# Edge sets sorted in groups of 1, 2, 2, 2 and 1 over later stretches of steps, and the residual scaled by GpSimd in the node phase

## The reference

```python
def gnn(h, src, edge_attr):                    # h = layernorm(x)
    node_feat = relu(h @ W_down.T + b_down)    # 256 -> 64
    time_feat = relu(edge_attr @ W_time.T + b_time)   # 32 -> 64, for every edge
    sums, counts = segment_sum(time_feat, src), segment_sum(1, src)
    mean = sums / maximum(counts, 1)
    fused = relu(concat(node_feat, mean) @ W_fusion.T + b_fusion)
    return h + (fused @ W_up.T + b_up)

x1 = x + gnn(layernorm(x), src, edge_attr)
out = x1 + ffn(layernorm(x1))                  # shared MLP + the best 2 of 4 experts
```

## Time and profile before

| | |
|---|---|
| median of 3 runs | 2168.73 us (2162.14 to 2173.69) |
| the profiled execution | 2177.41 us, of which the span of its trace is 2175.5 us |
| TensorE busy (PE) | 2000.5 us, 92% of the span |
| its weight loads (PEld) | 1672.3 us, 77% |
| VectorE (DVE) | 1779.5 us, 82% |
| ScalarE (ACT) | 1404.0 us, 65% |
| GpSimd (POOL) | 1069.4 us, 49% |
| transfers | 323.68 MB, 149 GB/s in the mean |
| chain that ended last | PE 71%, DVE 11%, DMA 5%, ACT 5%, issue 4% |

### The profile page before, as it was taken

How to read it: one execution, slowest core, us unless ns; L and a number is a source line. 1 busy time by engine, 2 the same in 40 slices (tenths; PEclk the granted TensorE clock), 3 DMA queues, 4 the chain that set the end, 5 groups by cost and what they waited for, 6 DMA issues and landing times.

```text
span 2175.5 us, 75498 instructions
## 1 busy us (share of the span) xinstructions
PE 2000.5 (92%) x26922; PEld 1672.3 (77%) x26946; DVE 1779.5 (82%) x5883; ACT 1404.0 (65%) x3239; POOL 1069.4 (49%) x918
## 2 busy tenths in 40 slices
PE   4788888999999999999999999677869999999998
PEld 1576776799988899999899999677756667666666
DVE  9788999899988999998788887688966767767675
ACT  2598898999989888888988887000014444444443
POOL 0577777778787777787777776100011111111110
PEclk7699999999999999999999999899989999999999
DMA  2244343677766677776778776676731111212110
GB/s 85 71 127 122 126 126 122 189 213 208 211 198 180 205 219 220 217 217 200 208 226 245 239 223 183 178 205 184 205 96 44 53 58 44 66 44 66 44 54 31
DMA packets 239411, 323.68 MB, mean 149 GB/s; under 512 B 42144, under 2 KB 213965, under 8 KB 238706
## 3 DMA queue, kind: packets, MB, share of 16 engines
q1 hardware_dynamic: 176564, 192.90, 32.6%
q0 software_dynamic: 41504, 103.41, 13.0%
q10 hardware_dynamic: 20970, 22.54, 3.7%
HBM read 186.34 MB, written 175.77 MB: 166 GB/s over the span
## 4 chain that ended last, share of the span: by engine, by line
PE 71%; DVE 11%; DMA 5%; ACT 5%; issue 4%; SPq 1%; DVEq 1%; ACTq 1%; POOL 1%; POOLq 0%
PE moved L686 16%; PE bank L715 15%; PE bank L803 10%; PE bank L672 7%; PE moved L816 7%; PE bank L690 4%; DMA arena<-table 3%; DVE arena L1133 2%; PE bank L843 2%; DMA table<-arena 2%; DVE arena L1134 2%; PE bank L699 2%; ACT arena L1590 1%; DVE arena L1334 1%; ACT arena L1596 1%
## 5 line engine op out<-in xcount | busy, mean ns | idle before, releaser
L1812 POOL DMA_INDIRECT table<-arena x832 | 970.3, 1166 | 377.2 <-issue 262.3
L1596 ACT ACTIVATE arena<-moved 128x588 bf16<-128x588 f32 x832 | 547.0, 662 | 108.2 <-PE moved L686 91.7
L686 PE MATMUL moved<-arena 128*128 128x196 bf16 x4992 | 590.5, 254 | 7.8 <-ACT arena L1596 6.7
L686 PEld LDWEIGHTS moved<-arena 128*128 128x128 f16 x4992 | 453.6, 98 | 79.8 <-ACT arena L1596 19.1
L1590 ACT ACTIVATE arena<-bank 128x512 f32<-128x512 f32 x624 | 371.0, 595 | 84.0 <-PE bank L672 68.0
L1235 DVE TENSOR_TENSOR sums<-sums,bank 128x130 f32 x816 | 232.0, 284 | 109.4 <-PE bank L715 88.9
L715 PE MATMUL bank<-arena 128*128 128x64 bf16 (+1 forms) x7344 | 273.4, 194 | 37.2 <-DVE sums L1235 24.6
L715 PE MATMUL bank<-arena,w_all 128*128 128x64 bf16 (+1 forms) x7344 | 272.4, 194 | 19.4 <-DVE sums L1235 18.9
L1711 ACT ACTIVATE arena<-bank,w_all 128x512 f32<-128x512 f32 (+1 forms) x225 | 152.8, 679 | 207.8 <-PE bank L803 116.6
L715 PEld LDWEIGHTS bank<-arena 128*128 128x128 bf16 x7344 | 254.7, 98 | 41.7 <-DVE arena L1215 41.7
L715 PEld LDWEIGHTS bank<-arena,w_all 128*128 128x128 bf16 x7344 | 254.2, 98 | 23.8 <-DVE w_all L1215 23.7
(11 more groups left out here) (292 smaller groups left out, 2864.8 us busy)
## 6 DMA issues: line engine op xcount, KB each, us to landing
arena<-table SPq DMA_DIRECT2D x672, 147.0 KB
arena<-in_attr SPq DMA_DIRECT2D x208, 144.0 KB
arena<-table ACTq DMA_DIRECT2D x144, 147.0 KB
table<-arena POOLq DMA_INDIRECT x832
...
```

The lines of the kernel that those rows point to most:

```text
L686: mm = e.matmul(moved8[:, 4 * (n % 2) + h, 0:PW], slot_hot[s % NSLOT][:, t, h * P:(h + 1) * P], upper(s, 0, PW)[:, t, :], start=j == 0, st ...
L1596: e.activation(row_buf[n % NROWS], moved8[:, 4 * (n % 2):4 * (n % 2) + 3, 0:PW], ACT.Copy).then_inc(s_rows, 1)
L1812: e.indirect_dma_start(out=table, out_offset=bass.IndirectOffsetOnAxis(ap=dest[s % NDEST][:, a:a + 1], axis=0), in_=row_buf[n % NROWS].rea ...
```

## The change

Two things change.

1. **The sorts.** The five sorts take 1, 2, 2, 2 and 1 sets instead of 1, 1, 2, 2 and 2. The second sort keeps its window (steps 1 to 19) and now has two sets in it; the third moves from steps 22 to 45 to steps 26 to 71, the fourth from 51 to 97 to 77 to 123, the last from 103 to 149 to 129 to 175 and has one set.
2. **The residual.** `x_ln`, its 98 stores and ScalarE's `xs_a` go. VectorE's `1 + r` and `s` of all tiles stay in SBUF (`rs_one`, `shift_all`). In the node phase SyncE reloads a group's tiles from `x`, the kernel's input, and GpSimd scales them, one `tensor_scalar` of 128x256 a tile, waits for its own result and then adds the bias as before. A load of a node tile in the loop now waits for the normalised tile in place of `xs_a`; the statistics write their unused output to `passed`; and `fused_a` has one buffer, whose next write waits for the previous store.

The code behind the sorts loses three lines, so that L1133 becomes L1130 and so on.

```diff
-SETS_OF_SORT = (1, 1, 2, 2, 2)
+SETS_OF_SORT = (1, 2, 2, 2, 1)
...
-        sort_windows = [None, (1, 20), (22, 46), (51, 98), (103, 150)]
+        sort_windows = [None, (1, 20), (26, 72), (77, 124), (129, 176)]
...
                         if a >= NXA:
-                            e.wait_ge(s_xs_a, a - NXA + 1)
+                            e.wait_ge(s_xn_a, a - NXA + 1)
...
-                    if name == "keep_x":
-                        e.wait_ge(s_xs_a, a + 1)
-                        e.dma_start(x_ln[g * P:(g + 1) * P, t * D:(t + 1) * D], xs_a).then_inc(s_xln[a % 2], 16)
...
             def load_xs(g):
                 if g >= 2:
                     e.wait_ge(s_x1, landed_x1(g - 2))
-                e.dma_start(xs[g % 2][:, 0:nt[g], :].rearrange("p t d -> p (t d)"), x_ln[g * P:(g + 1) * P, 0:nt[g] * D]).then_inc(s_xln_in[g % 2], 16)
+                full, r0 = full_tiles(g), g * TN * P
+                if full:
+                    e.dma_start(xs[g % 2][:, 0:full, :], x[r0:r0 + full * P, :].rearrange("(t p) d -> p t d", p=P)).then_inc(s_xs_in[g % 2], 16)
...
-                        e.activation(xn_a, xa[a % NXA], ACT.Identity, bias=shift_a[j % 2][:, i:i + 1], scale=rs_a[j % 2][:, i:i + 1]).then_inc(s_xn_a, 1)
-                        if a:
-                            e.wait_ge(s_xln[(a - 1) % 2], 16 * ((a - 1) // 2 + 1))
-                        e.activation(xs_a, xa[a % NXA], ACT.Identity, bias=shift_a[j % 2][:, i:i + 1], scale=rs_one[j % 2][:, i:i + 1]).then_inc(s_xs_a, 1)
+                        e.activation(xn_a, xa[a % NXA], ACT.Identity, bias=shift_all[:, a:a + 1], scale=rs_a[j % 2][:, i:i + 1]).then_inc(s_xn_a, 1)
...
-                        if j >= 2:
-                            e.wait_ge(s_fused_out[j % 2], 32 * (j // 2))
-                        e.activation(fused_a[j % 2], bank[MB][:, 256:384], ACT.Identity, bias=b_f).then_inc(s_fused_a, 1)
+                        if j:
+                            e.wait_ge(s_fused_out[(j - 1) % 2], 32 * ((j - 1) // 2 + 1))
+                        e.activation(fused_a, bank[MB][:, 256:384], ACT.Identity, bias=b_f).then_inc(s_fused_a, 1)
...
             def add_up_bias(g):
-                e.wait_ge(s_xln_in[g % 2], 16 * (g // 2 + 1))
+                e.wait_ge(s_xs_in[g % 2], landed(g, x_dmas))
                 xs_g = xs[g % 2][:, 0:nt[g], :]
+                for t in range(nt[g]):
+                    a = g * TN + t
+                    ins = e.tensor_scalar(xs_g[:, t, :], xs_g[:, t, :], rs_one[:, a:a + 1], shift_all[:, a:a + 1], ALU.mult, ALU.add)
+                ins.then_inc(s_xs_scaled, 1)
+                e.wait_ge(s_xs_scaled, g + 1)
                 e.tensor_tensor(xs_g, xs_g, b3r(b_u, nt[g], D), ALU.add).then_inc(s_xs_up, 1)
```

More of the change, by code:

```diff
@@ L91, in gnn_ffn @@
     fused_dram = nc.dram_tensor("fused_node", (NG * P, TN * P // 2), f32, kind="Internal").ap()
-    x_ln = nc.dram_tensor("x_ln", (NG * P, TN * D), f32, kind="Internal").ap()
     with ExitStack() as ctx:
@@ L109, in gnn_ffn @@
         s_x = [sem(f"s_x_in{i}") for i in range(NXA)]
-        s_xln = [sem(f"s_xln{i}") for i in range(2)]
-        s_xln_in = [sem(f"s_xln_in{i}") for i in range(2)]
+        s_xs_in = [sem(f"s_xs_in{i}") for i in range(2)]
         s_out = [sem(f"s_out{i}") for i in range(2)]
@@ L196, in gnn_ffn @@
         waiting = sb("waiting", [1, 1], f32)
-        ARENA = 31648
+        rs_one = sb("rs_one", [P, NT], f32)
+        shift_all = sb("shift_all", [P, NT], f32)
+        ARENA = 31440
         arena = sb("arena", [P, ARENA], f32)
@@ L290, in gnn_ffn @@
         xn_a = carve([D], f32)
-        xs_a = carve([D], f32)
+        passed = carve([D], f32)
         xt_a = [carve([K, P], f32) for _ in range(2)]
         nf_a = carve([P], f32)
-        fused_a = [carve([P], f32) for _ in range(2)]
+        fused_a = carve([P], f32)
         less_mean = [carve([2], f32) for _ in range(2)]
@@ L298, in gnn_ffn @@
         rs_a = [carve([2], f32) for _ in range(2)]
-        rs_one = [carve([2], f32) for _ in range(2)]
-        shift_a = [carve([2], f32) for _ in range(2)]
         used_1 = top[0]
@@ L418, in gnn_ffn @@
         node_at = {}
-        NODE_STEPS = {"load": 0, "stats": 1, "root": 2, "inverse": 3, "normed": 6, "keep_x": 7, "transposes": 7, "evacuate": 7, "down": 8, "down_relu": 8, "fuse": 9, "keep": 9, "store": 10}
+        NODE_STEPS = {"load": 0, "stats": 1, "root": 2, "inverse": 3, "normed": 6, "transposes": 7, "evacuate": 7, "down": 8, "down_relu": 8, "fuse": 9, "keep": 9, "store": 10}
         PAIRED = ("root", "inverse", "down", "down_relu", "fuse", "keep", "store")
@@ L588, in sync_program @@
                         for i in range(2):
[L589 removed]
+                            e.dma_start(fused_dram[row:row + A, i * P:(i + 1) * P], fused_a[i * A:(i + 1) * A]).then_inc(s_fused_out[j % 2], 16)
             for k, n in last_turns:
@@ L597, in load_xs @@
                     e.wait_ge(s_x1, landed_x1(g - 2))
-                e.dma_start(xs[g % 2][:, 0:nt[g], :].rearrange("p t d -> p (t d)"), x_ln[g * P:(g + 1) * P, 0:nt[g] * D]).then_inc(s_xln_in[g % 2], 16)
+                full, r0 = full_tiles(g), g * TN * P
+                if full:
+                    e.dma_start(xs[g % 2][:, 0:full, :], x[r0:r0 + full * P, :].rearrange("(t p) d -> p t d", p=P)).then_inc(s_xs_in[g % 2], 16)
+                if full < nt[g]:
+                    e.dma_start(xs[g % 2][0:rows[g][-1], full, :], x[r0 + full * P:N, :]).then_inc(s_xs_in[g % 2], 16)
                 if g >= 2:
@@ L606, in sync_program @@
             e.wait_ge(s_added, N_LOADS * CL)
-            for a in range(NT - 2, NT):
-                e.wait_ge(s_xln[a % 2], 16 * (a // 2 + 1))
             for j in range(NT // 2 - 2, NT // 2):
```

19 lines of the change are left out of this document (9 added, 10 removed).

## The result

The changed kernel took 2179.97 us in the median of 15 runs (2174.17 to 2188.04), beside 2168.74 us of 15 runs of the kernel before: a ratio of 1.0055, with a 95% interval of 1.0043 to 1.0067. It is slower by some 11 us. That lies in the predicted range (2159 to 2187), just beyond the 0.5% that I called the bound of a measurable change, and the sum of +3.7 us held only a third of it.

What follows compares the result with a forecast made beforehand. Bounds by stretch: VectorE in steps 1 to 7, 15 to 19, 29 to 35; ScalarE in 49 to 56; TensorE in 57 to 91 and the node phase. Sum +5.3 - 1.5 - 1.2 + 1.1 = +3.7 us: 2172.4, range 2159 to 2187.

Steps and rivals of the forecast that it cites:

- steps 1 to 7, 8 to 14, 15 to 19: Early main loop: more sort rows on VectorE cost +2.4 (+1.0 to +4.4), +0.8 (0 to 3), +3.8 us (2.5 to 5).
- steps 20 to 28: Main loop: 12.1 us fewer sort rows gain nothing, since TensorE's own 5.88 us a step stays: 0.
- steps 29 to 35: Main loop: fewer sort rows on VectorE, which sets the pace, give back -4.2 us (-6.9 to -1.5).
- steps 36 to 48: Main loop: sort rows ahead of size rows in steps 45 to 48 cost +1.0 us (0 to 2.1).
- steps 49 to 56, with the activation: Main loop, ScalarE full: one activation fewer saves time, limited by VectorE's added sort rows: -1.5 us (-3 to 0).
- steps 57 to 156, with the store's wait: Main loop: dropped stores' wait gives -1.2 us; TensorE, full in steps 77 to 91, absorbs lag there, 0 (0 to 3).
- steps 157 to 160: Before turns begin: 13.1 us more sort rows make VectorE 3.5 late, partly covered by a table-load wait: +1.5 us (0 to 3.5).
- step 207 to the second group: Node phase start: GpSimd's four scalings delay the first group by +1.1 us (0 to 2.1); later groups 0.
- Rival A: Node phase: GpSimd blocks VectorE in every group, deciding from about 0.63 us a scaling; about 2190 us, chance 0.10.
- Rival B: Early sort costs all 17.1 us of steps 1 to 19, only 1.5 return; +16.5 us, 2185, chance 0.10.
- Rival C: Relief reaches further: all 6.9 us return in steps 29 to 35, scatter waits vanish (-8); -11.1, 2157.6 us, chance 0.14.

Runs made afterwards that it cites:

- the second trace of before: The kernel before, run once more unchanged for a second trace: 2170.72 us.
- those steps charged: Changed kernel with 18 units of planner work added to every step from 49 on without a turn, so fewer sort rows stand there: 2175.49 us, ratio 1.0012.
- The doubled scalings: Changed kernel with each of the 98 GpSimd scalings followed by a second that multiplies by one and adds nothing: 2200.38 us in one run.

## Why the prediction was right in its range and short in its sum

I subtract the second trace of before from the trace after: 9.2 us in all. Outside the table lie -0.2 us in steps 161 to 206, -1.7 behind the second group, and the roundings.

| term | forecast | traces |
|---|---|---|
| steps 1 to 7, 8 to 14, 15 to 19 | +2.4, +0.8, +3.8 | +4.2, +0.9, +3.8 |
| steps 20 to 28 | 0 | +3.1 |
| steps 29 to 35 | -4.2 | -6.0 |
| steps 36 to 48 | +1.0 | -2.2 |
| steps 49 to 56, with the activation | -1.5 | +0.9 |
| steps 57 to 156, with the store's wait | -1.2 | +2.8 |
| steps 157 to 160 | +1.5 | +3.7 |
| step 207 to the second group | +1.1 | +0.2 |

*Right:* VectorE sets the pace in the early stretches, steps 15 to 19 pay their rows, steps 29 to 35 give back (within my bound of 6.9), the groups stay 22.4 us apart, and a scaling lies under 0.63 us.

*Luck:* that the time lies in the range. The range was wide, and the misses have both signs: steps 1 to 7, 20 to 28, 49 to 76 and 157 to 160 cost more than I had, steps 29 to 48 gave 5.0 us more.

*The step that failed* is how I set each stretch's extra rows against the idle time of the same stretch. Lateness isn't paid there. It is carried on to the first instruction for which TensorE needs VectorE, and the clock that TensorE loses behind the wait comes on top, for which I had no term. For steps 1 to 7 I let steps 6 and 7 take up almost half of the 4.4 us; 4.2 were paid, 3.1 of them in step 7. For "Steps 20 to 28: TensorE's own 5.88 us stays: 0" the sort ran on into step 20 and its first count came late: a wait of 2.1 us and some 1.2 by the clock, +3.1. For steps 157 to 160 I more than halved a lateness of 3.5 us, because VectorE had waited 3.90 us for a table load there; TensorE waited 3.1 and lost some 1.3 by the clock, less the 0.9 that the activation gave there (21.9 to 20.9 with the residual alone): +3.7.

Relief was carried on in the same way. For steps 36 to 48 I counted only the new rows in steps 45 to 48, +1.0, and -2.2 came. VectorE was busy 38.4 of 52.0 us in steps 36 to 44, before 47.9 of 52.6, so it came to the size phase of step 46 earlier: the wait of 3.5 us for its first rows fell to 0.9, and 2.4 were added at the next phase. These are TensorE's waits for VectorE from 330 to 376 us, around steps 45 to 48, before and then after.

```profile
PE bank L641 <- DVE arena L957: 3.5, 1, 3.5
```
```profile
PE bank L644 <- DVE arena L996: 2.4, 1, 2.4
PE bank L638 <- DVE arena L954: 0.9, 1, 0.9
```

For steps 49 to 56 the activation gave 1.7 us, as forecast (44.2 to 42.5 with the residual alone), but step 56, the first with a turn, took 8.25 us in place of 5.00. TensorE didn't wait for VectorE's piece there. What came late was ScalarE, which waited 3.2 us in step 56 for scatters to land, and TensorE for it. GpSimd, which issues the scatters, ran them back to back, two of them over 2.3 us long: ScalarE's two longer waits, and then GpSimd's rows.

```profile
416.58 0.66 ACT L1593 ACTIVATE arena<-moved 128x588 bf16<-128x588 f32 x1 [1.25 <-DMA table<-arena]
...
420.80 0.66 ACT L1593 ACTIVATE arena<-moved 128x588 bf16<-128x588 f32 x1 [1.64 <-DMA table<-arena]
```
```profile
415.44 2.57 POOL L1806 DMA_INDIRECT table<-arena  x1 [0.30 <-issue]
418.32 2.32 POOL L1806 DMA_INDIRECT table<-arena  x1 [0.30 <-issue]
```

In steps 49 to 56 27 scatter instructions took GpSimd 35.96 us, before 32 took 34.66, and 30 took 32.62 with those steps charged, when the stretch fell to 41.8 us. So the heap of sort rows does cost time there, but by way of ScalarE's waits for scatters. That VectorE's rows lengthen GpSimd's instructions goes with these counts, but wasn't tried.

The node phase's start was right in kind: from the end of the last addition of sums to the first L1486 it takes 8.9 us after, 7.0 and 7.2 in the two traces of before, +1.7 to +1.9 where I took +1.1 (0 to 2.1). The row in the table is smaller since the last turns happened to be shorter.

*Left out:* steps 57 to 76 took 3.2 us more after. That belongs to the sorts: these steps took 117.4 to 118.1 us in all six traces with the sorts of before and 119.7 to 123.9 in all seven with the changed ones. TensorE was busy throughout in both traces of before. After, ScalarE waited there for scatters to land, and TensorE for ScalarE.

```profile
ACT arena L1593 <- DMA table<-arena: 6.4, 8, 2.1
```
```profile
PE bank L687 <- ACT arena L1587: 3.6, 4, 1.7
```

With the sorts alone these scatter waits are 6.6 us in nine, with the residual alone there are none. Why the scatters land later isn't shown: VectorE has less work in these steps than before (98.8 us against 108.3).

*Rival A* was nearer than I gave it. The block exists, and moved L1524 by 0.62 us, the 0.6 that the prediction worked out; some 1.1 us were free, so it stayed hidden. In the first group L1524 took 1.88 us more, and the second group came 1.4 us later; how much of the one made the other isn't settled, since with the residual alone L1524 was as late (2.29 us) and the groups 23.3 us apart. The doubled scalings show the other side of the point. *Rival B* was half true: steps 1 to 28 paid 11.9 us of the 17.1, but 8.2 came back. *Rival C* fell: without the 98 stores ScalarE waited for scatters not less. Here are those waits in the second trace of before, and after.

```profile
ACT arena L1596 <- DMA table<-arena: 2.7, 3, 1.9
```
```profile
ACT arena L1593 <- DMA table<-arena: 13.2, 18, 2.1
```

In the earlier trace rows it was 8.0 us in six. So these waits differ by 5.3 us between the two traces of before, which differ by 6.6 in all. They don't hang on the stores: with the sorts alone, where the stores remain, they are 11.7 us in fifteen. With the changed sorts they are 10.3 to 13.2 us in all seven traces, with the sorts of before 2.7 to 15.1 in six; what else sets them wasn't tried.
